# A transformer block on one core: row maxima of the first two groups by key chunk, a lead of 34 units shrinking to 25, and another order of join, row transposition and tail

## What is computed

```python
x = x + 0.5 * ffn(layernorm(x), W_fc, ln_w, ln_b, W_proj)
x = x + attention(layernorm(x), wq, bq, wk, bk, wv, bv, wo, bo)
x = x + 0.5 * ffn(layernorm(x), W_fc, ln_w, ln_b, W_proj)
```

## Time and profile before

| | |
|---|---|
| median of 3 runs | 769.03 us (769.03 to 938.7) |
| the profiled execution | 770.04 us |
| its span | 767.9 us |
| mean granted clock of TensorE | 0.961 |
| PE busy | 727.3 us, 95% |
| DVE busy | 692.5 us, 90% |
| ACT busy | 637.5 us, 83% |
| POOL busy | 257.4 us, 34% |

### The profile page before, as it was taken

The page is one execution under the profiler, slowest core; times in us unless marked ns, Lnnn a source line. Parts: engine busy times, 40 slices in busy tenths (PEclk is TensorE's granted clock), DMA queues, the critical chain, the costliest instruction groups (busy, mean ns, idle before and its releaser), DMA issues.

```text
span 767.9 us, 17532 instructions
## 1 busy us (share of the span) xinstructions
PE 727.3 (95%) x6843; PEld 249.4 (32%) x6843; DVE 692.5 (90%) x880; ACT 637.5 (83%) x1196; POOL 257.4 (34%) x526
## 2 busy tenths in 40 slices
PE   6899779999999999999999999999999999999994
PEld 2774211222222222222222222222222222224473
DVE  5778659999999999999999999999999999996382
ACT  3443653899999999999999999999999999999742
POOL 4332001455445455233332222232222232425221
PEclk9999955999999999999999999999999999999997
DMA  7000000000011011011000000000000000000000
GB/s 219 2 1 0 1 1 1 3 4 5 24 25 25 24 25 25 25 24 40 4 4 5 4 4 4 6 17 5 4 4 4 5 7 20 8 6 4 5 29 28
DMA packets 22674, 12.45 MB, mean 16 GB/s; under 512 B 13088, under 2 KB 21152, under 8 KB 22336
## 3 DMA queue, kind: packets, MB, share of 16 engines
q1 hardware_dynamic: 11328, 8.77, 4.1%
q0 software_dynamic: 9056, 2.04, 1.6%
q10 hardware_dynamic: 2208, 0.53, 0.4%
HBM read 7.34 MB, written 2.33 MB: 13 GB/s over the span
## 4 chain that ended last, share of the span: by engine, by line
DVE 65%; PE 25%; issue 4%; ACT 3%; DMA 1%; DVEq 0%; POOL 0%; POOLq 0%; SPq 0%; ACTq 0%
DVE mh L818 59%; PE ps L1337 7%; PE ps L1324 5%; PE ps L1305 3%; PE ps L1124 2%; PE ps L1224 2%; PE ps L1183 2%; PE ps L1200 1%; DVE ring L680 1%; ACT KT L1029 1%; DVE top L826 1%; PE ps L1354 1%; DMA X<-in_L_attn_x_dram 1%; PE ps L1210 0%; DVE rope L843 0%
## 5 line engine op out<-in xcount | busy, mean ns | idle before, releaser
L818 DVE TENSOR_REDUCE mh<-ps 128x2 f32<-128x1024 f32 x512 | 584.9, 1218 | 7.0 <-PE ps L1305 6.9
L1080 ACT ACTIVATE ring<-ps 128x512 f32<-128x512 f32 x1024 | 551.5, 600 | 34.4 <-PE ps L1324 16.2
L1337 PE MATMUL ps<-ring,Vx 128*32 128x256 f32 x4096 | 325.6, 392 | 0.9 <-ACT outT L1088 0.9
L1305 PE MATMUL ps<-KT,QT 48*128 48x512 bf16 x1024 | 209.8, 393 | 10.6 <-DVE mh L818 10.4
L1324 PE MATMUL ps<-QT,KT 51*128 51x512 bf16 x1024 | 212.8, 389 | 1.1
L1337 PEld LDWEIGHTS ps<-ring,Vx 128*32 128x32 f32 x4096 | 82.1, 108 | 157.6 <-ACT ring L1080 142.1
L1324 PEld LDWEIGHTS ps<-QT,KT 51*128 51x128 bf16 x1024 | 51.8, 93 | 219.7 <-ACT ring L1080 205.2
L548 POOL DMA_DIRECT2D rope<-outT x80 | 43.1, 544 | 180.0 <-ACT outT L1088 171.1
L537 POOL DMA_DIRECT2D QT<-mrow x128 | 72.0, 568 | 42.0 <-DVE mrow L835 38.5
L1305 PEld LDWEIGHTS ps<-KT,QT 48*128 48x128 bf16 x1024 | 50.0, 94 | 67.1 <-DVE mh L818 30.2
L525 POOL TENSOR_TENSOR mp<-zeros,top 128x8 bf16<-128x8 f32 x32 | 6.4, 200 | 193.2 <-DVE top L826 193.2
(11 more groups left out here) (133 smaller groups left out, 351.8 us busy)
## 6 DMA issues: line engine op xcount, KB each, us to landing
rope<-rope_tables SPq DMA_DIRECT2D x2, 1024.0 KB, 6.1
QT<-mrow SPq DMA_DIRECT2D x128, 0.8 KB
QT<-mrow POOLq DMA_DIRECT2D x128, 0.8 KB, 1.7
rope<-outT SPq DMA_DIRECT2D x80, 8.0 KB
rope<-outT POOLq DMA_DIRECT2D x80, 8.0 KB, 1.7
q_bounce<-XB SPq DMA_DIRECT2D x3, 384.0 KB, 2.4
QT<-q_bounce SPq DMA_DIRECT2D x18, 64.0 KB
QT<-q_bounce POOLq DMA_DIRECT2D x18, 64.0 KB, 3.3
```

The source lines that it names most:

```text
L818: v.tensor_reduce(mh[:, n // A_STEP % 2, :, q, kb], ps[:, bank:bank + 2, :], AX.X, ALU.max)\
L1080: a.activation(ring[:, n % PRING, :], ps[:, exp_bank(n), :], ACT.Exp, scale=SCALE).then_inc(p_ready, 1)
L1305: mm = t.matmul(ps[:, A0 + 2 * (n % 2) + h, :], QT[rows, j, at:at + P], KT[rows, j, kb * CS:(kb + 1) * CS], start=True, stop=True)
L1337: mm = t.matmul(ps[r:r + 32, PO, 0:QH], Vx[:, kt, col:col + 32], ring[:, (2 * n + h) % PRING, half * QH:(half + 1) * QH], start=(kt == 0), ...
```

## The change

- **Order of the maxima.** Groups 0 and 1 are taken together by key chunk: four units of group 0 with K0, four of group 1 with K0, then both with K1, then group 0 with K2 and K3, then group 1 with K2 and K3 (`TURNS`, `ORDER`). Group 0 is complete after unit 23, not 15, and group 1 after unit 31. `row_max`, `max_mm` and the waits follow `ORDER` and `LAST_OF`.
- **Placing.** K1's odd half pair comes ahead of K2's even one in `PLACE_SEQ`, on ACT and on PE, and PE places every half behind a unit of its own. On ACT, the second cut of K3 stands behind the puts of K1 alone.
- **Lead.** 34 units of maxima come first (`LEAD_FIRST`). Then one pair of maxima in 28 units is left out (`LEAD_STEP`) until the lead is 25, after 9 x 28 = 252 units. Six warming matmuls stand ahead, behind units 28 to 33.
- **Whole maximum and transposition** come one unit later each (`TOP_AT`, `CUT_AT`).
- **End of the loop.** The first block of chunk 4's expansion moves ahead of group 31's last exponents (kind "H"), and the second one between the last value tiles.
- **Tail.** The last output product goes to bank 7 and ahead of the sums of squares; the last transposition ahead of the sums of squares of its step; on DVE the reciprocals go ahead of the first adds of squares, and the last adds ahead of the update in front of them; POOL computes the last layer norm's scale ahead of the first hidden scale.

```diff
...
 PV_LAG = 2
+LEAD_FIRST = 34
 LEAD = 25
+LEAD_STEP = 28
 PRING = 16
...
 
-CUT_AT = 2
+TOP_AT = 1
+CUT_AT = 3
 REC_AT = 6
...
 
+TURNS = ((0, 0), (1, 0), (0, 1), (1, 1), (0, 2), (0, 3), (1, 2), (1, 3))
+ORDER = [(g, q, kb) for g, kb in TURNS for q in range(CT)]
+ORDER += [(g, u % CT, u // CT) for g in range(2, NG) for u in range(A_STEP)]
+LAST_OF = [max(n for n, (of, _, _) in enumerate(ORDER) if of == g) for g in range(NG)]
+
+
 WIDE_FROM = (2 * (UNITS - LEAD) + 3) // 4 * 4
...
 LATE = {(NG - 2, 19): ("O", 0), (NG - 2, 23): ("O", 1), (NG - 2, 31): ("O", 2),
-        (NG - 1, 11): ("F", 0), (NG - 1, 15): ("F", 1), (NG - 1, 23): ("F", 2)}
+        (NG - 1, 11): ("F", 0), (NG - 1, 15): ("F", 1), (NG - 1, 23): ("F", 2), (NG - 1, 27): ("H", 0)}
 
...
 UNIT_SEQ = ("K0", "Q0", "K1", "Q1", "K2", "Q2", "K3", "Q3")
-PLACE_SEQ = (("K0", 0), ("Q0", 0), ("K1", 0), ("K0", 1), ("Q0", 1), ("K2", 0), ("K1", 1), ("K3", 0), ("K2", 1), ("K3", 1))
+PLACE_SEQ = (("K0", 0), ("Q0", 0), ("K1", 0), ("K0", 1), ("Q0", 1), ("K1", 1), ("K2", 0), ("K3", 0), ("K2", 1), ("K3", 1))
 UNIT_BANKS = 3
...
 
-            return late_tiles(A0 + c % 2 if c < NC - 1 else FC)
+            return late_tiles(A0 + c % 2 if c < NC - 1 else TP)
 
...
             sums(NG - 1)
+            ln_scale(2, NC - 1, NC - 1)
             hidden_scale(1, 0)
-            ln_scale(2, NC - 1, NC - 1)
             residual(1, NC - 1)
...
 
-                u = n % A_STEP
-                q, kb = u % CT, u // CT
+                g, q, kb = ORDER[n]
                 bank = A0 + 2 * (n % 2)
                 dve.wait_ge(a_ready, n + 1)
-                v.tensor_reduce(mh[:, n // A_STEP % 2, :, q, kb], ps[:, bank:bank + 2, :], AX.X, ALU.max)\
+                v.tensor_reduce(mh[:, g % 2, :, q, kb], ps[:, bank:bank + 2, :], AX.X, ALU.max)\
                     .then_inc(a_free, 1)
...
 
-                dve.wait_ge(a_free, (i + 1) * A_STEP)
+                dve.wait_ge(a_free, LAST_OF[i] + 1)
                 if i:
...
                     last_part("K3")
+                if n - TOP_AT in LAST_OF:
+                    whole_max(LAST_OF.index(n - TOP_AT))
+                if n - CUT_AT in LAST_OF:
+                    max_rows(LAST_OF.index(n - CUT_AT))
                 g, u = n // A_STEP, n % A_STEP
-                if u == A_STEP - 1:
-                    whole_max(g)
-                if g and u == CUT_AT - 1:
-                    max_rows(g - 1)
                 if g > PAIRS and g % PAIRS == 3 and u == REC_AT:
                     reciprocals(g // PAIRS - 1)
+            whole_max(NG - 1)
             max_rows(NG - 1)
...
 
-            add_squares(NC)
             reciprocals(NC - 1)
...
                             ALU.mult).then_inc(ot_ready, 1)
+            add_squares(NC)
+            output_chunk(NC - 1)
             variance(NC)
-            output_chunk(NC - 1)
+            norm_rows(2, X2, NC - 1, NC - 1)
             update(NC)
-            norm_rows(2, X2, NC - 1, NC - 1)
             add_squares(NC + 1)
+            take(NC - 1)
             variance(NC + 1)
-            take(NC - 1)
             update(NC + 1)
...
             variance(NC + 2)
+            add_squares(NC + 3)
             update(NC + 2)
-            add_squares(NC + 3)
             variance(NC + 3)
...
             second_cut("K2")
-            put("K2", 0, 0)
-            put("K2", 0, 1)
             put("K1", 1, 0)
...
             second_cut("K3")
+            put("K2", 0, 0)
+            put("K2", 0, 1)
             put("K3", 0, 0)
...
                 n, x = m // 2, m % 2
-                g, u = n // A_STEP, n % A_STEP
+                g, q, kb = ORDER[n]
                 j, c = g % PAIRS, g // PAIRS
-                h, q, kb = 1 - x, u % CT, u // CT
+                h = 1 - x
                 rows = slice(HR * h, HR * h + R_QK)
...
                         pe.wait_ge(v_free, NC)
-                    if g == 0 and q == 0:
-                        pe.wait_ge(place_ev, 2 * max(PLACE_SEQ.index((y, 0)) for y in ("Q0", f"K{kb}")) + 1)
-                    if g == 1 and u == 0:
+                    if g < 2 and q == 0:
+                        pe.wait_ge(place_ev, 2 * max(PLACE_SEQ.index((y, g)) for y in ("Q0", f"K{kb}")) + 1)
+                    if g == 2 and q == 0 and kb == 0:
                         pe.wait_ge(place_ev, 2 * len(PLACE_SEQ))
-                    if c and j == 0 and u == 0:
+                    if c and j == 0 and q == 0 and kb == 0:
                         for part in range(2):
...
                             pe.wait_ge(x2_ready, c - 1)
-                    else:
-                        pe.wait_ge(h_ready, (c - 2 + NC) * KH + 1)
                     for i in range(CT):
...
                     last.then_inc(o_ready, 1)
+                elif kind == "H":
+                    pe.wait_ge(taken, 2)
+                    expand_block(NC, 0)
                 else:
...
 
-            for n in range(LEAD):
+            for n in range(LEAD_FIRST):
                 max_mm(2 * n)
...
                 if n == 5:
+                    place_half("K1", 1, 0)
+                if n == 6:
+                    place_half("K1", 1, 1)
+                if n == 8:
                     place_half("K2", 0, 0)
+                if n == 9:
                     place_half("K2", 0, 1)
-                if n == 6:
-                    place_half("K1", 1, 0)
-                if n == 7:
-                    place_half("K1", 1, 1)
-                if n == 9:
+                if n == 11:
                     place_half("K3", 0, 0)
+                if n == 12:
                     place_half("K3", 0, 1)
-                if n == 10:
+                if n == 14:
                     place_half("K2", 1, 0)
-                if n == 11:
+                if n == 15:
                     place_half("K2", 1, 1)
-                if n == 12:
+                if n == 17:
                     place_half("K3", 1, 0)
-                if n == 13:
+                if n == 18:
                     place_half("K3", 1, 1)
-                if n > A_STEP:
+                if n > 27:
                     warm(1, EXP[1])
+            lead = LEAD_FIRST
             for g in range(NG):
...
                     exp_mm(g, k)
-                    if k % 2 and n + 2 * LEAD < 2 * UNITS:
-                        max_mm(n - 1 + 2 * LEAD)
-                        max_mm(n + 2 * LEAD)
+                    if k % 2 and lead > LEAD and n // 2 % LEAD_STEP == LEAD_STEP - 1:
+                        lead -= 1
+                    elif k % 2 and n + 2 * lead < 2 * UNITS:
+                        max_mm(n - 1 + 2 * lead)
+                        max_mm(n + 2 * lead)
                     if n < WIDE_FROM:
...
                         late(*LATE[g, k])
+            pv_tile(NG * NT - 4)
+            pv_tile(NG * NT - 3)
             pe.wait_ge(taken, NC - 1)
-            expand_block(NC, 0)
             expand_block(NC, 1)
-            for n in range(NG * NT - PV_LAG - 2, NG * NT):
-                pv_tile(n)
+            pv_tile(NG * NT - 2)
+            pv_tile(NG * NT - 1)
 
...
             contract(NC)
+            late("O", NC - 1)
             sum_squares(NC)
-            late("O", NC - 1)
-            for k in range(1, KH):
-                expand_block(NC + 2, k)
+            expand(NC + 2)
             pe.wait_ge(x2_ready, NC)
-            expand_block(NC + 2, 0)
             contract(NC + 1)
+            late("F", NC - 1)
             sum_squares(NC + 1)
-            late("F", NC - 1)
             contract(NC + 2)
...
```

## The result

The changed kernel is slower: 789.9 us in the median of four executions (785.0 to 793.4) against 769.3 before, a ratio of 1.026 with a 95% interval of 1.020 to 1.032. The profiled execution took 785.0 us with a span of 783.1. One execution of the kernel before took 938.7 us; it stands apart from all its others and is left out of the ratio. The forecast, 767.5 with a range of 761.0 to 770.5, missed by 22 us, and most of that lies in one place that no step of the forecast looked at.

A forecast was written before the change was run, and what follows sets the result against it. DVE's score maxima were taken to bound the kernel at 18.41 us a group, PE close behind at 18.18. +7.3 -5.4 -1.6 +0 -1.75 = -1.45 us gave 768.6, about 767.5 for the median, range 761.0 to 770.5.

The forecast's parts named there:

- Part 2: Sixth unit to unit 252, lead shrinking from 34 to 25: PE's pace of 18.06 us replaces 18.41 a group; -5.4 us.
- Part 3: Whole maximum one unit later: its 0.11 us wait goes in groups where DVE binds, -1.6 us; transposition stays covered.
- Part 1: The join at the start: DVE gets 5.3 us ahead, but exponents stand behind 34 units, not 25; +7.3 us.
- Rival E: In the join, single halves cost DVE 2.4 us more than worked out; 769.9 us; 5% chance.
- rival B: Clock up early: placed halves no longer hold DVE, exponents begin at about 131.5; 760.5 us; 7% chance.
- rival C: Long stretch: PE misses its own pace, score pairs wait for ACT; slower above 18.15 us a group; 772.9 us; 15%.
- Rival A: DVE stays the bound throughout and keeps most of its lead from the join; 761.2 us; 15% chance.
- rival D: The later whole maximum saves nothing, as waits between DVE's own instructions would be free; 769.1 us; 10% chance.
- Parts 4 and 5: Loop end: hidden block moved ahead, 0 us, bound +0.5. Last chunk: reordering 0, adds ahead of the update -1.75 us.

The follow-up runs named there:

- experiment 1: The changed kernel with GpSimd's cut of the next group's maximum ahead of the output DMAs of the group before; 771.6 us, ratio 1.0019 to the kernel before.
- 2: The changed kernel with a lead of 31 in place of 34 and a wait for the last placed half ahead of the first exponents; 768.5 us, ratio 0.9983.
- 3: The changed kernel with a lead of 32 and a wait for the last placed half ahead of the first exponents; a single execution, 771.3 us.
- 4: The changed kernel with DVE's transposition of groups 2 to 8 eight units behind the last maximum instead of three; 772.6 us, ratio 1.0034.
- 5: The changed kernel with GpSimd's cut between the wait for ACT's output copy and the four output DMAs; a single execution, 777.7 us.
- experiment 6: The kernel before with only the whole maximum and the transposition one unit later; 766.5 us, ratio 0.9952.
- the exchange: The kernel before with the new loop end and tail, but PE's sums of squares of the second block ahead of the last transposition; 767.9 us, ratio 0.9976.
- 8: The changed kernel with GpSimd's cut ahead of the output DMAs and PE's sums of squares ahead of the last transposition; 770.9 us, ratio 1.0021.
- 9: The kernel before with later whole maximum and transposition, new tail with sums of squares first, and ACT's cast of K3 ahead of K1's halves; 762.6 us, ratio 0.9900.

## Why the prediction was wrong

**The step that failed** is Part 2, where it says that with pairs left out PE's pace counts, and with it the last sentence of Part 3, that the transposition has the start of the group as its cover. Both ask when the rows are wanted. Neither asks what stands ahead of the cut on GpSimd. In positions: with a lead L, PE issues the last maxima of group g+1 at exponent unit 16g + 31 - L, and ACT copies group g-1 out at unit 16g + 1. GpSimd has the copy's DMAs first and the cut second. At L = 25 the maxima end at 16g + 6, five units behind the copy, and the order costs nothing. At L = 34 they end at 16g - 3, four units ahead of it. The transposition is three units on, the cut is ready 4.1 us behind the copy (157.12 to 161.2), and DVE waits the rest. Every unit by which the lead is longer is a unit of waiting per group; it fades as the lead shrinks, 4.25 to 0.60 us over six groups. Experiments 1 to 5 take this apart from each side: without the order (1), with less lead (2, 3), without the wait (4), with half of it (5).

**The join (Part 1)** was right in each term; the +7.3 was +6.7, counted from K2's last part, in every profile with a lead of 34. Rival E, dearer single halves, would have made it larger, and rival B, the clock up ahead of the exponents, did not come: full clock came back 6.2 us or more behind the first one.

**The pace (Part 2)**, once the queue is repaired (experiment 1): 18.15 us a group where 18.06 was forecast, so 4 rather than 5.4 us come back. The mis-sized term is the 0.21 us that a left-out pair was to give. In that run the scores of three units around one, and ACT's exponentials of one group:

```profile
199.90 0.39 PE L1334 MATMUL ps<-QT,KT 51*128 51x512 bf16 x2
...
200.79 0.57 PE L1334 MATMUL ps<-QT,KT 51*128 51x512 bf16 x2
...
202.08 0.39 PE L1334 MATMUL ps<-QT,KT 51*128 51x512 bf16 x2
```

```profile
176.14 17.69 ACT L1090 ACTIVATE ring<-ps 128x512 f32<-128x512 f32 x32
```

and, over 150 to 280 us, PE's weight loads for scores in the view of who waited for whom:

```profile
PEld ps L1334 <- ACT ring L1090: 45.5, 112, 0.4
```

The unit without maxima takes 0.89 us, as in the earlier trace rows, but the next one takes 1.29 in place of 1.11: PE's loads end a wait for ACT's exponentials in nearly every unit (up to 0.4 us each), and what PE is ahead in one unit is gone in the next. Two units take 2.18 in place of 2.22 us, so a left-out pair gives 0.04 us. So 18.18 us a group is the pace at which PE and ACT run together, not PE's alone. The prediction took the 0.90 from one unit at the end of the loop, where five banks are in use, and didn't ask whether the next unit keeps it.

18.15 is just rival C's point. Rival A, DVE as the bound throughout, is refuted by the same run: its groups are shorter than DVE's 18.28, and its time is 10 us above A's 761.2. Rival C's mechanism, a score pair that comes when ACT frees a bank, was present by 0.09 us a group and no more. The slower side came about, but by a mechanism that was not among the rivals.

**Part 3** was right: 0.13 us a group, against 0.11 forecast. The rule of the Trainium skill (VectorE: DVE Perf Modes, section The DRAIN you can't avoid) that a semaphore costs nothing extra, by which it should give nothing, was not borne out, neither here nor in experiment 6 by itself. The same section does say that a next instruction which is not held starts earlier, as the transposition does in the earlier trace rows. So rival D falls.

**Parts 4 and 5**: the end of the loop costs 0.4 us (last two copies 15.92 us apart, not 15.50), within its bound. The tail gains 2.2 us rather than 1.75 from copy to update; in three of seven profiles 1.65 of it is lost again to the half clock.

**What is left between the repaired kernel and the forecast** (770.9 against 767.5): some 1.4 us of pace, 0.4 at the end of the loop, 2.7 for PE's gap near 668 us with what follows it, against which stand 0.6 at the start and 0.8 in the tail (35.7 us with the exchange). That adds up to 3.1 of 3.4, but the clock at the start, which differs by some us from one execution to the next, is in both medians.

**What the sum hid.** It set the shrinking lead against 18.41, and gave the later whole maximum only the groups where DVE binds. That adds up, but it reads as if join and lead nearly paid for themselves. The later whole maximum alone brings every group to 18.28 (experiment 6), and against that the lead returns 0.13 x 15.4 = 2.0 us of the 6.7 that it costs at the start. Experiments 8 and 9 show the outcome: with the new order of maxima and the lead 770.9, without them 762.6. Both have the earlier cast; 2.7 us of the difference are PE's gap near 668 us.

## What to carry to other kernels

When a lead between two stages is changed, write down for each in-order engine, also those with little to do, where its list has the instruction of the leading stage and where that of the trailing one, and compare the positions at both leads; an engine busy for a third of the time can stop all others. An order that is free at one lead becomes a wait in every group at another, without any duration changing. And where two edits draw on the same slack between two engines, take them one after the other: the second has what the first has left.

## What the runs showed of the hardware

- Vector's wait for its own directly preceding result shows as 0.11 to 0.13 us, and vanishes with one instruction between (experiment 6).
- With a gap of PE of 1.3 us in the tail, three of seven profiles have the clock at half a few us behind it, and the 32 matmuls that follow take 5.46 us in place of 3.8. With a gap of 0.5 us none of three has it. In the loop, of the three longest gaps (3.71, 2.58 and 2.57 us) the first and the third had half clock behind them and the second had not.
- After the join, full clock came back 6.2 to 11.7 us behind the first exponent in twelve profiles, with no order by kernel: 9.5, 9.5, 11.6, 6.2 and 11.7 with the old lead, 6.2, 6.2, 6.2, 7.8 and 9.7 with a lead of 34. The first output copy stands 21.9 to 24.0 us behind the first exponent by it.
